# A 16-graph attention network on one core: graphs staggered one per three slots, weights loaded each slot, spent heads moved into the next slot's first product, half of the heads turned through memory

## What is computed

```
for l in range(3):                                  # first network
    scores = leaky(x @ w[l,:256] [:,None] + x @ w[l,256:] [None,:] + b[l], 0.2)
    attn = softmax(where(adj + eye > 0, scores, -inf))
    h = layernorm(x + attn @ x, g1[l], beta1[l])
    x = layernorm(h + gelu(h @ W1[l] + b1[l]) @ W2[l] + b2[l], g2[l], beta2[l])   # 256 -> 1024 -> 256
x = layernorm(x_in + x)
xh = (x @ W_proj) split into 8 heads of 32          # second network
att = softmax(where(adj > 0, leaky(a_src[:,None] + a_dst[None,:] + b), -1e30))    # 512 x 512 for each head
out = layernorm(x + relu(att @ xh))
```

## Time and profile before

| | |
|---|---|
| median of 3 runs | 2322.04 us (2321.35 to 2323.39) |
| the profiled execution | 2323.47 us |
| its span, first to last instruction | 2321.7 us |
| TensorE busy | 2213.5 us, 95% |
| vector engine busy | 1809.9 us, 78% |
| ScalarE busy | 1684.1 us, 73% |
| moved to and from memory | 219.30 MB |
| mean granted TensorE clock | 0.985 of full speed |

### The profile page before, as it was taken

One profiled execution on the slowest core, in us unless ns is written; L12 is line 12 of the kernel. 1 busy time (PEld: TensorE's weight loads), 2 busy tenths in 40 slices (PEclk: granted clock), 3 DMA queues, 4 the chain that ended last, 5 costly groups with the idle time before them and its releaser, 6 DMA issues.

```text
span 2321.7 us, 32320 instructions
## 1 busy us (share of the span) xinstructions
PE 2213.5 (95%) x10501; PEld 1560.0 (67%) x10501; DVE 1809.9 (78%) x5722; ACT 1684.1 (73%) x3243; POOL 201.1 (9%) x200
## 2 busy tenths in 40 slices
PE   3999999999999999999999999999999999999976
PEld 2676767766776677677677667766776776777643
DVE  5457587779788787887788787887878878766778
ACT  2433468776778778787787777787778877888796
POOL 0010110000100010001100001000010011001100
PEclk9999999999999999999999999999999999999978
DMA  6011024343163232532443421632316323200111
GB/s 219 11 37 55 10 96 135 93 150 101 46 197 109 76 127 54 188 105 63 133 130 103 153 90 58 188 104 89 124 47 199 97 65 104 69 19 19 37 42 37
DMA packets 115874, 219.30 MB, mean 94 GB/s; under 512 B 7768, under 2 KB 57212, under 8 KB 110332
## 3 DMA queue, kind: packets, MB, share of 16 engines
q1 hardware_dynamic: 115708, 217.24, 29.8%
HBM read 164.52 MB, written 52.69 MB: 94 GB/s over the span
## 4 chain that ended last, share of the span: by engine, by line
PE 75%; DVE 16%; ACT 5%; issue 3%; POOL 1%; DMA 0%; SPq 0%; DVEq 0%; POOLq 0%; ACTq 0%
PE ffn L1240 21%; PE av L1157 14%; PE ffn L1229 11%; PE av L1229 11%; PE pT L1140 8%; PE av L1181 4%; DVE prob L777 2%; DVE prob L768 2%; PE av L1216 2%; ACT xs L555 1%; DVE lone L729 1%; POOL rstd L469 1%; PE trow L1119 1%; DVE xs L903 1%; DVE stats L716 1%
## 5 line engine op out<-in xcount | busy, mean ns | idle before, releaser
L1240 PE MATMUL ffn<-w_sb,G 128*128 128x256 f32 x3072 | 741.1, 381 | 0.0
L1240 PEld LDWEIGHTS ffn<-w_sb,G 128*128 128x128 f32 x3072 | 561.3, 191 | 90.3 <-issue 24.3
L777 DVE CUSTOM_DVE_ANT_0 prob<-trow,mask 128x512 f32<-128x512 f32 x676 | 439.3, 686 | 34.3 <-PE trow L1119 19.4
L1229 PE MATMUL ffn<-hT,w_sb 128*128 128x512 f32 x768 | 355.0, 595 | 1.1 <-ACT hT L534 1.1
L1140 PEld LDWEIGHTS pT<-ident,prob 128*128 128x128 f32 x2032 | 255.9, 143 | 148.0 <-issue 101.6
L1229 PE MATMUL av<-hT,w_sb 128*128 128x512 f32 x768 | 353.5, 593 | 0.0
L469 POOL TENSOR_TENSOR rstd<-veps,mhalf 128x4 f32<-128x4 f32 x127 | 167.2, 1317 | 2082.9 <-DVE veps L712 2082.9
L515 ACT ACTIVATE prob<-prob,s 128x512 f32<-128x512 f32 x484 | 331.5, 716 | 2.4 <-DVE nm L784 1.8
L1140 PE MATMUL pT<-ident,prob 128*128 128x128 f32 x2032 | 312.1, 278 | 20.0 <-DVE prob L840 7.6
L521 ACT ACTIVATE prob<-prob,nm 128x512 f32<-128x512 f32 x448 | 317.7, 712 | 0.0
L1157 PE MATMUL av<-xs,prob 128*128 128x257 f32 x1024 | 244.3, 380 | 3.9 <-ACT prob L526 3.9
(11 more groups left out here) (154 smaller groups left out, 2727.2 us busy)
## 6 DMA issues: line engine op xcount, KB each, us to landing
w_sb<-in_L_gnn_W SPq DMA_DIRECT2D x48, 1024.0 KB, 8.4
blocks_dram<-blocks SPq DMA_DIRECT2D x168, 256.0 KB, 4.2
prob<-blocks_dram SPq DMA_DIRECT2D x42, 1024.0 KB, 4.8
trow<-rows_dram SPq DMA_DIRECT2D x127, 256.0 KB, 3.2
adj_sb<-in_adj SPq DMA_DIRECT2D x16, 1024.0 KB, 7.0
xin<-in_x SPq DMA_DIRECT2D x16, 512.0 KB, 6.3
x0r<-in_x SPq DMA_DIRECT2D x16, 512.0 KB, 5.8
out<-o SPq DMA_DIRECT2D x15, 512.0 KB, 3.3
```

Source lines behind the costliest of these rows:

```text
L777: return v.tensor_tensor_reduce(out=out_[:, t, :], in0=targets, in1=mask[:, t, :], scale=1.0, scalar=LEAST, op0=ALU.add, op1=ALU.max, accu ...
L1229: last = te.matmul(ff1[f % len(ff1)][:], w1_sb[:, g // 2 % STAGES, dt, f * P:(f + 1) * P], hT[:, dt, :], start=dt == 0, stop=dt == DT - 1)
L1240: last = te.matmul(ffn[part][:, at:at + D], G[:, f, t * P:(t + 1) * P], w2_sb[:, g // 2 % STAGES, f, :], start=f == 0, stop=f == FT - 1)
```

## The change

Graphs are staggered: from the sixth slot on, each group of three slots holds the last layer of one graph, the middle layer of the next and the first layer of the one behind it, so one graph ends in each third slot. The slots are called here by what they hold: g % 3 = 2 *opening* (three heads made; keep_masks; graph_begins), g % 3 = 0 *ending* (two heads made; graph_sum, graph_out, make_masks for a later graph, two heads turned in blocks), g % 3 = 1 *hand-over* (three heads made; the next graph's residual norm, projection and targets). The first graph's heads are made four in slot 6 and four in slot 7. There are 49 units instead of 48: the loop ends with slot 45; slot 46 has no attention; then the attention of the last unit stands alone; then the last feed-forward part; then the heads from 115 on (before: from 111 on).

```
-MADE_IN_SLOT = [3, 3, 3, 3, 2, 2]
-BY_BLOCKS = (1, 2, 4, 5, 8, 10, 13)
+MADE_IN_SLOT = {2: 3, 0: 2, 1: 3}
+FIRST_MADE = {LAYERS * 2: HEADS // 2, LAYERS * 2 + 1: HEADS // 2}
+BY_BLOCKS = (1, 2, 4, 6)
...
 def unit_of(u):
-    return u // SLOTS, u % SLOTS % 2, u % SLOTS // 2
+    if u < len(FIRST_SLOTS):
+        return FIRST_SLOTS[u]
+    return [(u // 3 - 1, 2), (u // 3, 1), (u // 3 + 1, 0)][u % 3]
...
+def weights_of(u):
+    return u // 2 if u < len(FIRST_SLOTS) else u - 2 - (u > BUBBLE)
...
 def moved(q):
-    return q < LAST_HEADS - 2 * HEADS and q % (2 * HEADS) in BY_BLOCKS
+    return q < LAST_HEADS - 2 * HEADS + 3 and q % HEADS in BY_BLOCKS and q >= HEADS
```

SyncE loads a set of weights in each slot, when the second product of the slot before has ended:

```
-                if g % 2 == 0 and g and g + 2 < UNITS:
+                if g > 1 and weights_of(g) != weights_of(g - 1):
+                    u = next(u for u in range(g + 1, UNITS) if u != BUBBLE and weights_of(u) > weights_of(g))
                     sp.wait_ge(s_ff2, PARTS * g)
-                    load_weights(g // 2 + 1)
+                    load_weights(u)
```

The vector engine's slot, behind the attention:

```
                 for q in turned_behind(g)[:1]:
                     turn_blocks(q)
-                if done is not None and done % 2 == 0:
+                if done is not None:
                     graph_sum(done)
...
                 if done is not None:
                     graph_out()
-                fed_forward(s, 0)
-                if k == 2:
+                fed_forward(graph, 0)
+                if g == 3:
                     keep_masks(0)
-                if k == 3 and p < PAIRS - 1:
                     make_masks(0)
-                if k == SLOTS - 1:
-                    keep_masks(1)
-                    if p < PAIRS - 1:
-                        make_masks(1)
+                elif g > 3 and g % 3 == 2:
+                    keep_masks(g // 3 % 2)
+                elif g > 3 and g % 3 == 0 and g // 3 + 1 < GRAPHS:
+                    make_masks((g // 3 + 1) % 2)
                 for q in new[2:]:
                     head_made(q)
                 for q in turned_behind(g)[1:]:
                     turn_blocks(q)
-                fed_forward(s, 1)
+                fed_forward(graph, 1)
```

TensorE's slot (`four` is the first of the heads spent):

```
+                ahead, inside, behind = (4, (1, 1), (1, 1, 1, 1)) if four is None else (2, (2, 1), (2, 1, 2, 1))
...
                 for f in range(FT):
-                    if f == FT - 2:
+                    if f == (FT - 2 if four is None else FT - 3):
                         first_target_row()
                     first_product(g, f)
+                    if f == 1 and four is not None:
+                        attend_heads(four)
+                    if f == 3 and four is not None:
+                        heads_back(four)
```

More of the change, by code:

```diff
@@ L588, in _ @@
             held = []
-            for g in range(UNITS - 1):
-                p, s, l = unit_of(g)
-                _, s2, l2 = unit_of(g + 1)
+            for g in range(REGULAR):
+                l = unit_of(g)[1]
+                graph2, l2 = unit_of(g + 1)
                 new, heads = made(g), turned(g)
-                place, four = side_by_side(heads)
-                begin, ends = begun(g), first_ends(g)
+                four, begin = spent_at(g), begun(g)
                 for f in range(FT):
@@ L618, in _ @@
                         exponential(q, t)
-                if place == 0:
-                    head_rows(four)
                 for t in range(T):
@@ L633, in _ @@
                         values_out(begin, t)
-                    if t == 0 and place == 1:
-                        head_rows(four)
                     if t == 1:
@@ new lines, in _ @@
+            plus_bias(GRAPHS - 1, 1)
+            head_made(second)
+            for t in range(T):
+                turned_out(first - 1, t)
+            fed_forward(GRAPHS - 1, 0)
+            head_made(third)
+            for t in range(T):
+                turned_out(first, t)
+            fed_forward(GRAPHS - 1, 1)
+            layer_ends(GRAPHS - 1, 1)
+            dve.wait_ge(s_hn, c("hn"))
+            dve.sem_inc(s_passed, 1)
+            scores(GRAPHS - 1, LAYERS - 1)
+            heads_out(first - 5)
@@ new lines, in _ @@
+            first_targets(1)
+            graph_begins(GRAPHS - 2)
+            for t in range(T):
+                head_targets(third + 1, t)
+                if t < T // 2:
+                    first_exponents(2 * t)
+                    first_exponents(2 * t + 1)
+            head_maxima(third + 1)
+            attention(GRAPHS - 1, LAYERS - 1, third + 2)
+            heads_out(first - 1)
+            graph_sum(GRAPHS - 3)
+            head_made(third + 3)
+            times_gain(GRAPHS - 1, LAYERS - 1)
@@ L1315, in _ @@
                             turn(q, f - T)
-                for t in range(T):
-                    piece(t)
-                attention(s2, l2, g + 1, lambda i: piece(4 + i))
-                if place == 0:
-                    attend_heads(four)
+                pieces(ahead)
+                attention(graph2, l2, g + 1, lambda i: pieces(inside[i]))
                 for t in range(T):
@@ L1326, in _ @@
                         state_in(begin, t - T + DT)
-                    piece(6 + t)
-                if place == 0:
-                    heads_back(four)
+                    pieces(behind[t])
                 for t in range(T):
-                    for q in heads[2:3]:
+                    for q in heads[2:]:
                         if not moved(q):
```

537 lines of the change are left out of this document (279 added, 258 removed).

## The result

The changed kernel takes 2481.14 us in the median (2478.05 to 2481.67 in its timed runs) against 2322.29 us before: 1.068 times the time (95% interval 1.066 to 1.070). Three single executions, one of this kernel (2988 us at a mean granted TensorE clock of 0.749; it was the profiled one), one of e10 (2376 us) and one of e11 (10919 us), took longer than the others of their kernel and stand in no median here, so that what follows is read from a second trace of the changed kernel, 2479.46 us (span 2477.7, clock 0.970).

A forecast was written before the change was run, and what follows sets the result against it. TensorE's own instructions were taken to set the time; -14.0 - 13.3 + 114 + 5.2 + 14.3 + 8 + 17.1 = +131.3 us on the 2321.7 us span gave 2453 us, range 2390 to 2515.

The forecast's parts named there:

- the clock: TensorE's lower clock after stalls in hand-over slots: bounds nothing and 5 us a cycle (60), taken as nothing.
- the start: Slot 6 makes four heads and the masks: 6 us of stall, plus 2 for slot 3, +8 us.
- head 6's way back: Head 6 returns through memory late for the spent heads; TensorE waits 1.1 us x 13, +14.3 us.
- the normalise: State's transposes in ending slots wait for ScalarE's normalise, 0.4 us x 13, +5.2 us.
- The ending slot: Vector engine's 22.2 us behind the attention bring part 1 11.4 late; TensorE stands 9.5 us in twelve cycles, +114 us.
- The rule that I had set beside it: Each of the 12 stalls is followed by a cold, slow-clock stretch on TensorE, some 20 us in all.
- The rival in which the weights issued behind it slow it down: Head 6's load shares memory with 2 MB of weights, up to +47 us; part of the more-lost case, chance 0.17.
- The weights: 22 more sets of two 1 MB weight loads, one set each slot, covered by a 43 us slot: nothing.
- -14.0: Eight more heads go by memory instead of being turned on TensorE, 8 x 1.75 us off, -14.0 us.
- The end: From slot 46 on, including the last unit's lone attention: 227.5 us against 210.4, +17.1 us (bounds 0 to 35).
- the 5.1 us of table loads: ScalarE changes functions in the last first product: eight loads of 1.28 us, half on the path, 5.1 us.
- My rival of the other side: Ending slot fits: the 114 us and head 6's 14 go, 2325 us, or 2308 with smaller terms reduced; chance 0.09.

The follow-up runs named there:

- e10: On top of e9, head 109 turned ahead of the last unit's target row and head 115 copied by ScalarE: 2338.48 us.
- e11: On top of e9, head 2's block turn back in the ending slot, hand-over scores ahead of the layer's end: 2329.91 us.
- e2: Changed kernel with the graph's sum and its statistics ahead of the ending slot's attention instead of behind it: 2421.24 us.
- e3: Changed kernel with the masks ahead of the ending slot's attention instead of behind part 0: 2455.40 us.
- e5: On top of e4, the masks' first two instructions moved to where the vector engine waits ahead of the ending slot's attention: 2375.39 us.
- e4: On top of e2, head 2 of each graph turned in blocks ahead of the hand-over slot's attention, not in the ending slot: 2421.86 us.
- e9: On top of e7 plus times_gain moved behind the hand-over attention: third and fourth heads in slots 7 and 8 use a PSUM bank each; 2334.41 us.
- e7: On top of e6, ScalarE's four exponentials behind the eight gelu in the last first product, two function changes instead of eight: 2351.46 us.
- e6: On top of e5, spent heads one f later in ending slots, and their way back one f later too: 2354.78 us.

## Why the prediction held, and where its sizes were off

The forecast of 2453 us was 28 us too low and inside its range. Of the 28, the clock and the start make some 10 each and head 6's way back 5.5; a forecast 5.2 for the normalise did not come; the rest is not traced.

**The ending slot.** This step carried the forecast, and its numbers stand, with what the trace shows in brackets: 22.2 us of work behind the attention (22.0), TensorE through after 10.8 (10.5), 11.4 late (11.5), the target row 9.5 behind (9.5). Only, TensorE does not stand for all of the 9.5: the waits shown above come to 85.3 us, 7.1 a cycle, and the rest went into slow products. The opening slot took 45.3 us (45.4 was said), the ending slot without the stand behind it 45.2 (44.7), the hand-over slot with that stand 54.0 to 55.7 (54). The experiments show the cause, not only the place: moving vector work out of that stretch, with the work itself unchanged, took time away (e2, e3, e5; in e4 the wait came back in another place), and once enough of it was gone (e5) the waits of slots 9 to 45 at f = 0, f = 3 and the target row were none.

**The clock** was taken at nothing, and that term was mis-sized. Of the 12 hand-over slots five took 50.9 us, six about 52.5 and one 51.4, with the target row at 17.6 us in the first two kinds; the difference is TensorE at a lower clock behind the row. One of the long ones and the stretch behind its target row (1391.04), by windows:

```profile
1373.44:1425.98 52.54, 48.32 (x200) 34.13 (x201) 43.13 (x134) 31.08 (x61) 3.98 (x5) 0.94 0.44 135
...
1391.90:1395.30 3.40, 3.40 (x10) 1.58 (x9) 3.33 (x11) 0.18 (x1) 0.00 (x0) 0.62 0.99 394
```

Over the twelve that is some 10 us (six of 1.6 and one of 0.5). What TensorE loses ahead of the row costs nothing, since the row waits for the vector engine in any case. The rule that I had set beside it (the Trainium skill, TensorE: Matmul & The Clock Gate, section HAM oscillation) gave 20 us, a cold start behind every stall. The trace agrees in that each of the twelve slots has a slow stretch: TensorE is busy for 46.4 to 48.3 us in them, against 45.15 in e4's slot above at the full clock. But only some half of the slots paid for it.

**Head 6's way back**: 1.4 to 1.6 us in ten of the cycles and 2.6 in two, where 1.1 was forecast, 19.8 in all instead of 14.3. The rival in which the weights issued behind it slow it down fell: the load was issued at 1180.66 and its products start at 1185.61, 4.95 us, with 2 MB of weights issued from 1182.65 on; the median landing is 4.9, against 4.8 before. In all twelve cycles the products start 4.9 to 5.1 us behind the issue; in the two with 2.6 us the load itself was issued 1.2 us later in the slot. The Trainium skill (DMA: Bandwidth & Descriptors, section Queues, rings and completion order) says that each memory engine takes the work of one queue in order, and the trace agrees as far as it goes: the loads behind did not hold up the one ahead.

```profile
1180.66 0.34 SPq L394 DMA_DIRECT2D prob<-blocks_dram  x1
...
1182.65 0.43 SPq L347 DMA_DIRECT2D w_sb<-in_L_gnn_W  x1
```

**The normalise** (+5.2) did not come: no transposes of states waited in slots 9 to 45. **The weights** cost nothing, as forecast. **The start** is the other mis-sized term. From the first slot to slot 9 it took 402.4 us against 373.9 before (first row of the next view). Of these 28.5 us more, 10.5 are six heads that TensorE now turns there and not later (96 instructions more), which the sum has in its -14.0; 18 are left where 8 were forecast. The stand at slot 7 was 4.0 us instead of 6, slot 3 cost nothing (slots 0 to 5 took 243.0 us, 244.5 before), and the term lacked the 11.7 us of waits for ScalarE's copies in slots 7 and 8, most of which e9 took away. **The end** was 228.4 us for 227.5 forecast, which is luck in part: the slot without an attention and the lone attention took 81.2 (78.7 forecast), the last feed-forward part 42.9 (38.0), the rest 104.4 (110.8); of the 5.1 us of table loads e7 found 3.3.

**What the staggering itself is worth** is seen in e9, where nearly nothing waits in the middle. Start to slot 9, slots 9 to 45, and the rest, of the kernel before and of e9:

```profile
53.63:427.48 373.85, 362.77 (x1528) 259.21 (x1529) 246.68 (x793) 200.12 (x343) 32.58 (x30) 0.99 0.21 67
427.48:2111.29 1683.81, 1668.18 (x7986) 1178.37 (x7985) 1367.36 (x4344) 1307.18 (x2526) 149.74 (x147) 1.00 0.34 104
2111.29:2321.70 210.41, 167.94 (x929) 110.67 (x927) 165.69 (x479) 166.53 (x361) 15.94 (x14) 0.88 0.11 35
```

```profile
53.80:444.24 390.44, 374.37 (x1625) 267.61 (x1626) 244.42 (x813) 220.99 (x389) 33.22 (x30) 0.99 0.16 55
444.24:2108.65 1664.41, 1646.62 (x7794) 1161.98 (x7792) 1389.20 (x4355) 1283.53 (x2479) 129.54 (x148) 1.00 0.45 142
2108.65:2332.80 224.15, 163.38 (x893) 107.23 (x891) 160.39 (x454) 152.89 (x329) 12.54 (x13) 0.87 0.18 57
```

The middle is 19.4 us shorter: TensorE has 192 instructions less there (7986 - 7794), as many as the turning of twelve heads; the start is 16.6 us longer, because the first graph's eight heads come in two slots (six of the twelve are turned there instead), and the end 13.7, which the prediction put down to the last unit's lone attention; no run took that apart. Together they leave e9 11 us slower: with nearly all of its waits gone, the staggering wins nothing here. My rival of the other side, 2325 without the overrun and head 6's wait, was too low: e6, with neither, took 2354.8, of which some 21 are the attention's new wait, and e11's 2329.9 has the 16 us of e7 and e9 in it besides.

What stays open: how much of e9's 1.3 us inside the attention could go without a loss elsewhere (e11 took 0.4 of it), and whether the lone attention at the end could be filled with the work of the slot ahead of it, which was tried with one head only (e10).

## What to carry to other kernels

Count the work of an engine from the last thing it must wait for to the thing that others wait for, in the very slot, and hold it against the bound engine's work over the same stretch: an engine that is idle for a quarter of the span can still be the one that ends a slot last. Work without a due time (a sum, a mask) belongs where its engine waits anyway; moved there, unchanged, it gave back 60 (e2) and 46 us (e5) of 159. Where its engine has no room, the wait only moves along with it (e3 in part, e4). And ask of each lateness what hangs on it: putting the scores ahead of the layer's end made 4.3 us of it free.

## What I had not expected of the hardware

The same stand did not bring the lower clock at the same place each time. In e2 every hand-over slot has the stand of 2.76 us at f = 3; in eight of the twelve the two f's behind it ran slowly (5.2 us, in one 6.6 at a mean clock of 0.62, instead of 3.4), in four they did not, and the products behind the target row did. In e4, with stands of 0.57, 2.23 and 1.84 us in a slot and work between them, ten of the twelve slots have no slow stretch (granted clock 1.00) and two have one behind the target row (0.97 over the slot). The changed kernel ran its hand-over slots at two lengths, 50.9 and 52.5 us, and once at 51.4, though the target row came at the same time in both kinds. What decides where the stretch falls, no run here shows.
